# Attention block with a 4-bit feed-forward: scale maxima from flat copies, ordered copies and norm scales later, a new order

## What is computed

```python
q = rms_norm(layernorm(x), q_norm_w); k = rms_norm(ctx, k_norm_w); v = ctx
q, k = rotary(q), rotary(k)                 # 16 query heads, 4 key heads, 32 columns each
attn = softmax(causal(q @ k.T / sqrt(32)))
x = x + (attn @ v) @ w_out.T
h = layernorm(x)
w_up, w_down = ((w_q - 7.5) * repeat(scale, 64, axis=1)).T      # 4-bit weights held as int32
y1 = h @ w_up + b_up + h @ up_lora_a @ up_lora_b                # 512 -> 2048
y2 = relu(y1) @ w_down + b_down + relu(y1) @ down_lora_a @ down_lora_b
x = x + y2
```

## Time and profile before

| | |
|---|---|
| median of 3 runs | 485.68 us (484.91 to 486.22) |
| the profiled execution's own time | 485.92 us |
| its span | 484.1 us |
| busy: PE, DVE, ACT, POOL | 442.8, 352.2, 300.2, 282.2 us |
| DMA | 70.17 MB, mean 145 GB/s |

### The profile page before, as it was taken

One profiled execution on the slowest core, in us unless ns is written; L12 is line 12 of the kernel. 1 busy time (PEld: TensorE's weight loads), 2 busy tenths in 40 slices (PEclk: granted clock), 3 DMA queues, 4 the chain that ended last, 5 costly groups with the idle time before them and its releaser, 6 DMA issues.

```text
span 484.1 us, 8263 instructions
## 1 busy us (share of the span) xinstructions
PE 442.8 (91%) x2416; PEld 217.4 (45%) x2416; DVE 352.2 (73%) x1078; ACT 300.2 (62%) x927; POOL 282.2 (58%) x304
## 2 busy tenths in 40 slices
PE   0266859999999999999999999999999999999997
PEld 0254535444444444444444444444444444444443
DVE  3999898979879786868686877778777856544341
ACT  1599788877848575758575766667575846522120
POOL 5367677776758584838484747565666745351100
PEclk9996699999999999999999999999999999999999
DMA  5686869779866877988777687887678677474422
GB/s 147 258 261 142 190 208 213 134 146 144 169 130 123 167 118 154 130 174 123 162 134 152 132 168 131 169 126 159 125 144 158 115 151 113 91 122 97 88 56 74
DMA packets 207372, 70.17 MB, mean 145 GB/s; under 512 B 196912, under 2 KB 199728, under 8 KB 206688
## 3 DMA queue, kind: packets, MB, share of 16 engines
q1 hardware_dynamic: 205760, 69.09, 71.6%
q10 hardware_dynamic: 1488, 0.40, 0.4%
q0 software_dynamic: 80, 0.16, 0.1%
HBM read 16.95 MB, written 4.19 MB: 44 GB/s over the span
## 4 chain that ended last, share of the span: by engine, by line
PE 78%; DVE 1%; DMA 1%; SPq 0%; issue 0%
PE ff L936 33%; PE ff L922 32%; PE tb L904 7%; PE sb L876 2%; PE tb L892 2%; DMA x<-hid 1%; SPq L393 0%; PE tb L862 0%; DVE t_sin L1147 0%; DVE pr L1179 0%; DVE y L1229 0%; DVE stats L1160 0%; DVE x L1157 0%; DVE q L1188 0%; DVE wd_lo L1081 0%; DVE q L1096 0%
## 5 line engine op out<-in xcount | busy, mean ns | idle before, releaser
L936 PE MATMUL ff<-wd_hi,x 128*128 128x512 f16 x512 | 152.3, 379 | 0.6 <-DMA x<-hid 0.6
L922 PE MATMUL ff<-wu_hi,xnT 128*128 128x512 f16 x512 | 152.5, 379 | 0.2 <-ACT wu_lo L641 0.2
L679 ACT ACTIVATE pr<-pr,nmax 128x128 f32<-128x128 f32 x256 | 99.1, 389 | 14.6 <-DVE nmax L1179 13.9
L505 POOL TENSOR_TENSOR big<-pr,big 128x512 f16<-128x512 f32 x64 | 80.9, 1271 | 33.6 <-ACT big L710 33.5
L922 PE MATMUL ff<-wu_lo,xnT 128*128 128x512 f16 x256 | 97.0, 379 | 0.0
L936 PE MATMUL ff<-wd_lo,x 128*128 128x512 f16 x256 | 97.0, 379 | 0.0
L496 POOL TENSOR_TENSOR pr<-pr,rinv 128x512 f32<-128x512 f32 x64 | 72.7, 1137 | 35.7 <-DVE rinv L1089 35.7
L744 ACT ACTIVATE hid<-z 128x512 f16<-128x512 f32 x64 | 39.9, 624 | 80.5 <-DVE z L1110 80.5
L1179 DVE CUSTOM_DVE_ANT_0 pr<-sb,tabs,score_scale 128x128 f32<-128x128 f32 x256 | 73.8, 344 | 12.3 <-PE sb L876 11.2
L922 PEld LDWEIGHTS ff<-wu_hi,xnT 128*128 128x128 f16 x512 | 48.0, 98 | 58.9 <-issue 5.9
L1110 DVE SCALAR_TENSOR_TENSOR z<-ff,su,b_row 128x512 f32<-128x512 f32 x64 | 47.6, 744 | 36.0 <-PE ff L922 34.7
(11 more groups left out here) (149 smaller groups left out, 652.2 us busy)
## 6 DMA issues: line engine op xcount, KB each, us to landing
xt<-in_x SPq DMA_DIRECT2D x16, 256.0 KB, 3.1
big<-in_L_ffn_w_up_q SPq DMA_DIRECT2D x4, 1024.0 KB, 5.6
big<-in_L_ffn_w_down_q SPq DMA_DIRECT2D x4, 1024.0 KB, 6.3
out<-y SPq DMA_DIRECT2D x16, 256.0 KB, 2.7
kvt<-in_ctx SPq DMA_DIRECT2D x16, 64.0 KB, 2.9
wd_lo<-in_L_xattn_w_out SPq DMA_DIRECT2D x1, 1024.0 KB, 7.9
pT<-big SPq DMA_TRANSPOSE x64, 3.5
b_row<-in_L_ffn_b_up SPq DMA_DIRECT2D x1, 1024.0 KB, 9.2
```

Source lines behind the costliest of these rows:

```text
L505: pool.tensor_tensor(p3[:, m, :, 1, :], pr[:, m], p3[:, m, :, 0, :], ALU.subtract).then_inc(p_low, 1)
L679: last = act.activation(pr[:, m, g, :], pr[:, m, g, :], ACT.Exp, bias=nmax[:, p, j:j + 1], scale=-1.0, accum_out=rsum[:, p, j:j + 1])
L922: last = pe.matmul(bank[:], a[:, m, :], b[:, m, 512 * g:512 * g + 512], start=(m == 0 and i == 0), stop=(m == KC - 1 and i == 2))
L936: last = pe.matmul(ff[down_bank[n]][:], x2T[:, part, k + h % HG, :], b[:, h, :], start=(h == 0 and i == 0), stop=(h == HC - 1 and i == 2))
```

## The change

1. The maxima of the up scales, the down factor A and the bias are taken from flat copies (`s_up_flat`, `a_dn_flat`, `b_flat`), which lie in the third slot of the weight ring and are loaded in the memory's own order: 512 and 1024 bytes per partition, and 16 rows of 512 bytes. The copies in the tiles' order are loaded later: `s_up` in four pieces (one before and three after weight group 0), the down factor A in slot 137. So `lora_a_high` and `lora_a_low` are split in two, and a fourth scaling, `later_scales`, is added. Group 2 now waits until the maxima are taken.
2. SP loads weight group 0 without waiting; `ctx` 0 and the tables in two parts (identity first) are issued by ACT.
3. On DVE only the two maxima of the norm weights stay in the head; the norm scales and the first batch's moments move behind the first tile of weights. The bitwise and is made per column there.
4. `take_tops` is merged into `find_scales`, whose steps go from 17 to 13, ten of them before the LoRA factors can be scaled.
5. All order tables are new (one is shown); DVE has 25 instead of 27 of the tiles to dequantize (POOL 7 instead of 5) and 28 instead of 25 of the low parts (ACT 4 instead of 7). `sines` waits for the batch before.

```diff
-SCALE_STEPS = 17
+SCALE_STEPS, LORA_STEPS = 13, 10
...
-R_MOMENTS = (0, 23, 473, 1390)
+R_MOMENTS = (20, 77, 760, 1674)
...
-DVE_TILES = (0, 1, 2, 3, 4, 5, 6, 7, 8, 9, 10, 12, 13, 14, 15, 16, 17, 18, 19, 20, 22, 23, 24, 25, 27, 28, 30)
-LOW_BY_DVE = (0, 1, 2, 5, 9, 10, 11, 14, 15, 16, 17, 18, 19, 20, 21, 22, 23, 24, 25, 26, 27, 28, 29, 30, 31)
+DVE_TILES = (0, 1, 2, 3, 4, 5, 6, 7, 8, 9, 11, 12, 13, 14, 15, 17, 18, 20, 21, 24, 25, 26, 28, 29, 31)
+LOW_BY_DVE = (0, 1, 4, 5, 6, 8, 9, 10, 11, 12, 14, 15, 16, 17, 18, 19, 20, 21, 22, 23, 24, 25, 26, 27, 28, 29, 30, 31)
...
+LORA_A_AT, LORA_ALOW_AT = (3, 62), (2, 145)
+LORA_D_LOAD_AT, NORM_SCALES_AT = 137, 19
...
+        s_up_flat, a_dn_flat = big[:, 4096:4096 + HC * C // QB], big[:, 4224:4224 + HC * R]
+        b_flat = big[0:HC, 4480:4480 + P]
...
             def load_group(g):
                 if g >= W_RING:
                     sp.wait_ge(w_turned, 4 * (g - W_RING + 1))
+                if g == 2:
+                    sp.wait_ge(tops_ready, 7)
                 src = wuq_v[g] if g < 4 else wdq_v[g - 4]
                 sp.dma_start(stage_i[:, g % W_RING], src).then_inc(wq_in[g % W_RING], 16)
 
...
                 sp.dma_start(out[n], y[:, n % 2, :]).then_inc(y_out[n % 2], 16)
 
             sp.dma_start(s_dn[:], wds.rearrange("(p c) b -> p c b", p=P)).then_inc(scales_in, 16)
+            sp.dma_start(a_dn_flat, wda.rearrange("(p c) r -> p (c r)", p=P)).then_inc(lora_a_in, 16)
+            sp.dma_start(xt[:, 0, :], x[0]).then_inc(x_in[0], 16)
             sp.dma_start(qw_bc, qw.rearrange("(a n) -> a n", a=1).broadcast_to([P, C])).then_inc(q_weight_in, 16)
             sp.dma_start(kw_bc, kw.rearrange("(a n) -> a n", a=1).broadcast_to([P, CK])).then_inc(k_weight_in, 16)
-            load_batch(0)
-            sp.wait_ge(lora_a_in, 16 * 3)
-            sp.wait_ge(k_weight_in, 16)
-            sp.wait_ge(q_weight_in, 16)
+            sp.dma_start(s_up[:, 0:4, :].rearrange("p i b -> p (i b)"), wus_v[0]).then_inc(up_scales_in[0], 16)
             load_group(0)
+            for g in range(1, 4):
+                sp.dma_start(s_up[:, 4 * g:4 * g + 4, :].rearrange("p i b -> p (i b)"), wus_v[g]).then_inc(up_scales_in[1], 16)
             sp.wait_ge(parts_empty, 2)
             for s in range(SLOTS):
                 n = at(s, R_KTURN)
...
+                    sp.dma_start(a_nat[:, KC * R:].rearrange("p (g a) -> p g a", a=4 * R), wda_v).then_inc(a_dn_in, 16)
                 if s == WO_LOAD_AT:
                     sp.dma_start(wo_raw, wo.rearrange("(j p) c -> p j c", p=P)).then_inc(wout_in, 16)
                 if s == ROW_LOAD_AT:
...
         @block.scalar
         def _(act):
-            act.dma_start(s_up[:].rearrange("p (g i) b -> p g (i b)", i=4), wus.rearrange("(g p i) b -> p g (i b)", p=P, i=4)).then_inc(scales_in, 16)
-            act.dma_start(a_nat[:, KC * R:].rearrange("p (g a) -> p g a", a=4 * R),
-                          wda.rearrange("(g p i) r -> p g (i r)", p=P, i=4)).then_inc(lora_a_in, 16)
+            act.dma_start(s_up_flat, wus.rearrange("(p c) b -> p (c b)", p=P)).then_inc(scales_in, 16)
             act.dma_start(a_nat[:, 0:KC * R], wua.rearrange("(p c) r -> p (c r)", c=KC)).then_inc(lora_a_in, 16)
-            act.dma_start(b_nat[:], bu.rearrange("(p a) -> p a", p=P)).then_inc(lora_a_in, 16)
-            act.dma_start(tabs[:], tabs_d).then_inc(consts_in, 16)
+            act.dma_start(b_flat, bu.rearrange("(p a) -> p a", p=HC)).then_inc(lora_a_in, 16)
+            act.dma_start(tabs[:, 0:P], tabs_d[:, 0:P]).then_inc(ident_in, 16)
+            act.dma_start(tabs[:, P:], tabs_d[:, P:]).then_inc(consts_in, 16)
+            act.dma_start(kvt[:, 0, :], ctx[0]).then_inc(kv_in[0], 16)
 
...
                 dve.memset(tops[:], 0.0).then_inc(tops_zero, 1)
                 dve.wait_ge(tops_zero, 1)
                 dve.wait_ge(scales_in, 16 * 2)
-                top(0, s_up[:].rearrange("p a b -> p (a b)"))
+                top(0, s_up_flat)
                 top(1, s_dn[:].rearrange("p a b -> p (a b)"))
                 dve.wait_ge(b_flat_in, 16 * 2)
                 top(4, b_up_flat)
                 top(5, b_dn_flat)
                 dve.wait_ge(lora_a_in, 16 * 3)
                 top(2, a_nat[:, 0:KC * R])
-                top(3, a_nat[:, KC * R:])
-                top(6, b_nat[:])
-
-            def norm_powers():
+                top(3, a_dn_flat)
+                top(6, b_flat)
+
+            def norm_tops():
                 dve.wait_ge(q_weight_in, 16)
                 dve.wait_ge(k_weight_in, 16)
                 for j, w in enumerate((qw_bc, kw_bc)):
                     norm_link(dve.tensor_reduce(wmax[:, j:j + 1], w, AXX, ALU.max, apply_absolute_value=True), wait=False)
+
+            def norm_scales():
                 dve.wait_ge(norm_scale_steps, 2)
-                norm_link(dve.tensor_scalar(wmax[:], wmax[:], 1e-12, None, ALU.add))
-                norm_link(dve.tensor_scalar(wpow2[:].bitcast(I32), wmax[:].bitcast(I32), 0x7F800000, None, ALU.bitwise_and))
-
-            def norm_scales():
-                norm_link(dve.tensor_tensor(wsq[:], wpow2[:], wpow2[:], ALU.mult))
+                for j in range(2):
+                    norm_link(dve.tensor_scalar(wmax[:, j:j + 1], wmax[:, j:j + 1], 1e-12, None, ALU.add), wait=j > 0)
+                for j in range(2):
+                    norm_link(dve.tensor_scalar(wpow2[:, j:j + 1].bitcast(I32), wmax[:, j:j + 1].bitcast(I32), 0x7F800000, None,
+                                                ALU.bitwise_and), wait=j > 0)
                 for j, (unit, mul, add) in enumerate(((Q_TOP, 1.0 + EPS, EPS * EPS), (K_TOP, 1.0 / CK, EPS))):
-                    norm_link(dve.tensor_scalar(arg_mul[:, j:j + 1], wsq[:, j:j + 1], mul / unit ** 2, None, ALU.mult), wait=False)
-                    norm_link(dve.tensor_scalar(arg_add[:, j:j + 1], wsq[:, j:j + 1], add / unit ** 2, None, ALU.mult), wait=False)
+                    pw = wpow2[:, j:j + 1]
+                    norm_link(dve.tensor_scalar(arg_mul[:, j:j + 1], pw, pw, mul / unit ** 2, ALU.mult, ALU.mult), wait=False)
+                    norm_link(dve.tensor_scalar(arg_add[:, j:j + 1], pw, pw, add / unit ** 2, ALU.mult, ALU.mult), wait=False)
                 norm_link(dve.tensor_scalar(score_scale[:], wpow2[:, 0:1], wpow2[:, 1:2], SC / (Q_TOP * K_TOP), ALU.mult, ALU.mult))
 
...
-            def take_tops():
+            def find_scales():
+
+                bound, power, lora, deq = tmp[:, 0:5], tmp[:, 5:10], tmp[:, 10:12], tmp[:, 12:14]
                 dve.wait_ge(tops_spread, 1)
+                link(dve.tensor_scalar(deq, tb[0][:, 0:2], 7.5 / W_TOP, 1e-30 / W_TOP, ALU.mult, ALU.add), wait=False)
+                link(dve.tensor_scalar(lora, tb[0][:, 2:4], float(R) / W_TOP, None, ALU.mult), wait=False)
+                link(dve.tensor_scalar(bound[:, 2:4], tb[0][:, 2:4], 1e-30, 1.0 / A_TOP, ALU.add, ALU.mult), wait=False)
                 dve.tensor_scalar(tops_all[:], tb[0][:, 0:8], 1.0, None, ALU.mult).then_inc(tops_taken, 1)
-
-            def find_scales():
                 dve.wait_ge(tops_taken, 1)
...
-                for dst, src, wait in ((wpow, wtop, False), (apow, atop, False), (ytop[:, 1:2], ytop[:, 0:1], True)):
-                    link(dve.tensor_scalar(dst.bitcast(I32), src.bitcast(I32), 0x7F800000, None, ALU.bitwise_and), wait)
...
+                dve.wait_ge(scale_steps, 3)
+                for j in range(2):
+                    link(dve.tensor_scalar(bound[:, j:j + 1], lora[:, j:j + 1], tops_all[:, 4 + j:5 + j], deq[:, j:j + 1], ALU.mult, ALU.add), wait=j > 0)
+                link(dve.tensor_scalar(bound[:, 4:5], bound[:, 0:1], float(C) * W_TOP, tops_all[:, 6:7], ALU.mult, ALU.add))
+                link(dve.tensor_scalar(power.bitcast(I32), bound.bitcast(I32), 0x7F800000, None, ALU.bitwise_and))
+                link(dve.reciprocal(kap[:, 0:5], power))
+                for j in range(2):
+                    link(dve.tensor_scalar(kap[:, 6 + j:7 + j], kap[:, j:j + 1], power[:, 2 + j:3 + j], None, ALU.mult), wait=False)
+                assert step[0] == LORA_STEPS
+                dve.wait_ge(up_scales_in[0], 16)
+                dve.tensor_scalar(s_up[:, 0:4, :], s_up[:, 0:4, :], kap[:, 0:1], None, ALU.mult).then_inc(scales_ready, 1)
+                dve.tensor_scalar(s_dn[:], s_dn[:], kap[:, 1:2], None, ALU.mult).then_inc(scales_ready, 1)
+                link(dve.tensor_scalar(kap[:, 5:6], kap[:, 4:5], X2_TOP, None, ALU.mult))
+                link(dve.tensor_scalar(su[:], power[:, 0:1], kap[:, 5:6], -1.0 / XN_SCALE, ALU.mult, ALU.mult), wait=False)
+                link(dve.tensor_scalar(sd[:], power[:, 1:2], power[:, 4:5], 1.0 / X2_TOP, ALU.mult, ALU.mult), wait=False)
                 assert step[0] == SCALE_STEPS
                 dve.wait_ge(scales_ready, 2)
 
...
+            def later_scales():
+                dve.wait_ge(up_scales_in[1], 16 * 3)
```

(15 more changed lines are left out.)

219 lines of the change are left out of this document (106 added, 113 removed).

## The result

| | before | changed |
|---|---|---|
| median of 13 runs each | 485.68 us (484.06 to 487.15) | 487.92 us (486.56 to 489.26) |
| ratio, 95% interval | | 1.0043 [1.0028, 1.0058] |
| profiled execution: own time, span | 485.92, 484.1 us | 489.08, 487.3 us |

**Slower by 0.43%**; forecast were 483.9 us and a range that ended at 487.2. The profiled execution lies 1.2 us above its median. A second measurement of the unaltered changed kernel, on another chip, gave 1.0015 [1.0001, 1.0029]: the sign holds, but only just, and the size differs between chips by more than the intervals say.

The account below looks back on a forecast made before the run. DVE's queue sets when PE becomes continuous, and the end follows. Terms -2.4, -2.7, +3.6 and -0.65 put the first UP 2.1 us earlier and the end 1.8 us earlier: 483.9 us, range 481.2 to 487.2.

Parts of the forecast that it names:

- The end moves with the first UP: Whole kernel: the end moves as the moment PE becomes continuous does; forecast shift of the end -1.8 us.
- Rival 3: Repeated batches: new order tables leave a gap, 0.1 us in each of 13 batches; 485.2 us, chance 0.08.
- Term A: Head, wait for the maxima's data: factors B land earlier, -2.4 us, middle between nothing and 4.8 us.
- Term B: Head, from PE's turn of the maxima to the scaled tables: 6.3 us instead of 9.0, so -2.7 us.
- Term C: DVE work now ahead of the first UP: norm scales, moments, masks, low parts, fewer dequantizations; +3.4 us, 0.2 for fourth scaling.
- the low part it names: DVE's low part freeing the bank of the last tile but one ahead of the first UP; released at 71.89 us before.
- Rival 2: Early weights: weight group 1, behind the copies of factor B's rows, lands late and DVE waits; 487.4 us, chance 0.15.
- First UP: -2.4 - 2.7 + 3.6 - 0.65 = -2.1 us: First UP comes at 71.1 us; the last summand is one tile left after the bank's release instead of two.
- My list of edits costed at nothing: Split of `lora_a_high`, later load of down factor A, wait of `sines`, group 2's wait for the maxima: 0 us each.
- the sign by which it would be wrong: Forecast wrong if the head is faster but not the first UP, or first UP 2 us early without the end following.
- the forecast 1.8: End of the kernel: -1.8 us, between -1.4 at PE's last wait and -2.1 at the first UP.

Follow-up runs that it names:

- b3: Kernel before, with six more 128x512 reductions on DVE in the head; 488.50 us, 1.0052 of the kernel before.
- e10: Changed kernel with `b_row` loaded early, plus six more 128x512 reductions on DVE in the head; 488.25 us, 1.0051 of the kernel before.
- b1: Kernel before, with weight group 6 and `b_row` issued right ahead of the third batch's transpose of `q`; 493.08 us, 1.0136 of the kernel before.
- e4: Changed kernel, with SP's waits put back ahead of weight group 0; 486.84 us, 1.0011 of the kernel before.
- e6: Changed kernel, with `b_row` loaded early and SP's waits put back ahead of weight group 0; 483.70 us, 0.9954 of the kernel before.
- e1: Changed kernel, with `b_row` loaded ahead of the second batch's transpose (slot 390 instead of 797); 484.36 us, 0.9957 of the kernel before.
- c_row_early_again: Changed kernel, with `b_row` loaded early, measured again on another chip; 484.25 us, 0.9967 of the kernel before.
- e8: Changed kernel, with `b_row` loaded early and weight group 6 issued behind the transpose of `xn` (slot 866); 485.64 us, 1.0007 of the kernel before.

## Why the prediction was wrong

**The end moves with the first UP: right.** From the first UP to the end of the span the traces show 410.9 us before, 411.5 changed, 410.2 changed again, 410.0 and 410.2 with `b_row` early, 410.3 and 411.1 in b3 and e10. The exceptions are the runs that put a stall behind the first UP, above all `b1` with 417.0. Rival 3, a gap in the repeated order, did not occur: 99.25 us of 100 busy.

**Term A, -2.4 us: right.** Measured -2.76 (-2.4 to -3.0 in the three other traces of this head, changed again and `b_row` early). The middle between bounds of 0 and 4.8 was a choice for want of a row, so that it came this close is partly luck. The rule of the Trainium skill (DMA: Bandwidth & Descriptors, "Queues, rings and completion order") that each DMA engine serves its queues in turn, by which the gain would be nothing, was not decisive where it was weighed: the factor B landed 2.64 us earlier. But group 0 did slow the norm weights, by some 0.6 us (e4, e6 against the changed kernel).

**Term B, -2.7 us: right, the gain if anything larger.** From PE's turn to the scaled tables 5.5 us in the changed trace instead of the 6.3 forecast, and 5.7 to 6.3 in the other three. The bitwise and that was put at 1.3 us took 0.24, and 0.90 to 1.03 in the others. **Term C** had the norm scales and moments at 3.1 us; they took 15.74 - 13.93 = 1.8. Both were priced by instructions that had been held up, see below. Its count was off by one: up to the low part it names DVE dequantizes 22 tiles before and 18 now, four fewer and not three, another 0.9 us.

**The sum of these terms held on DVE.** It puts that low part (of tile 18) -2.4 - 2.7 + 3.6 = -1.5 us from 71.83, or -2.4 with four tiles counted; it was out at 69.55 in the changed trace, -2.3, and at 69.1 to 69.8 in the other three:

```profile
68.28 1.27 DVE L1103 TENSOR_TENSOR wd_lo<-ff,wd_hi 128x512 f16<-128x512 f32 x2
```

PE didn't come to its tile until 74.50, behind the scores.

**Rival 2, group 1 late: did not occur.** Issued at 18.51 instead of 20.6, it was there when DVE came to it at 24.52 us, since the two loads issued there took 5.9 and 7.7 us.

**The step that failed** is "First UP: -2.4 - 2.7 + 3.6 - 0.65 = -2.1 us". It counted DVE's work ahead of the first UP, took it that PE then had one tile left, and not what the new tables also moved: on PE the third batch's scores went ahead of the first UP (slots 1348 and 1463; before 1363 and 1244), so that transposes of `q` and `k` became its condition; in SP's row these transposes went directly behind weight group 5, `b_row` and group 6 (764, 797, 817, then 829 and 854), where before there were 7 us of pause; and `xn`'s, ahead of them before (1258, then 1271 and 1275), went behind them (865). No run puts the scores back behind the first UP, so the two ways on which the hold reaches it, by the scores and by `xn`, are not told apart; in the changed trace the scores came last. My list of edits costed at nothing didn't hold this, and only for group 1 (rival 2) did I ask what a load's new place in SP's row does. The prediction named the sign by which it would be wrong, a faster head without a faster first UP, and that is what came. In place of -2.1 us the profile shows +2.6: PE idle for 5.53 us, then two groups of scores, two tiles and the beginning of the first UP at half clock. With only that load elsewhere the same head and tables give -0.43 and -0.33% (`e1`, `c_row_early_again`), and -0.46% with group 0 waiting too (`e6`): 1.6 to 2.2 us, around the forecast 1.8. That they meet the forecast is in part luck, as the head gained more than forecast and these runs still wait for transposes. The stall costs the rest: 0.61% on one chip (1.0015 to `e6`'s 0.9954, which differs in group 0's waits too), and over all pairs from 0.48% (1.0015 to 0.9967) up to 0.86% (1.0043 to 0.9957, on different chips).

The head gained more than was forecast, though: the first tile 7.6 to 8.3 us earlier than in the trace before, factor B's step 4.6 to 5.3 us, and even with `b_row` early the first UP only 0.4 to 1.6 us. The traces show where it went. DVE has more to do between factor B's step and the low part of tile 18, 52.6 and 53.3 us with `b_row` early against 50.7 before, as the first batch's rotary steps moved behind it and four masks and three low parts were added, for four tiles fewer: of the 4.6 us 2.1 to 2.7 are left there. The rest goes on PE: in `e1` it still waits 1.9 us for scores and 1.2 us for `xn`, with weight group 6 in flight until 64.1, and in `c_row_early_again` 1.8 us for scores, and then it works at the lower clock. `e8` shows that 1.1 us of it goes with the load and comes back later.
